# Local attention of a fused decoder: dividing the exponentials by their sums before they are turned, instead of the results after

## What is computed

```python
qkv = h @ wqkv                                  # 256 -> 3 x 512, 8 heads of 64
q = l2norm(q) * qs ; k = l2norm(k) * ksc
q, k = rotary_xpos(q, k)
# windows of 128 tokens, each looks at itself and at the window before
sim = einsum('bhwid,bhwjd->bhwij', bq * 8.0, bk)
mask = (i < j) | (i > j + WINDOW) | (j == -1)
attn = softmax(where(mask, -max, sim))
o = einsum('bhwij,bhwjd->bhwid', attn, bv)
x = x + o @ wo
```

## Time and profile before

| | us |
|---|---|
| median of 3 runs (lowest, highest) | 2656.38 (2656.29, 2656.98) |
| the profiled execution, first to last instruction | 2656.6 |
| PE busy | 2298.0 (87%) |
| DVE busy | 1419.3 (53%) |
| ACT busy | 1042.2 (39%) |
| POOL busy | 696.8 (26%) |

### The profile page before, as it was taken

How to read it: one execution, slowest core, us unless ns; L and a number is a source line. 1 busy time by engine, 2 the same in 40 slices (tenths; PEclk the granted TensorE clock), 3 DMA queues, 4 the chain that set the end, 5 groups by cost and what they waited for, 6 DMA issues and landing times. The chain is left out here.

```text
span 2656.6 us, 38842 instructions
## 1 busy us (share of the span) xinstructions
PE 2298.0 (87%) x12968; PEld 1651.9 (62%) x12968; DVE 1419.3 (53%) x4229; ACT 1042.2 (39%) x2653; POOL 696.8 (26%) x669
## 2 busy tenths in 40 slices
PE   7994499988869969995698899698999898999898
PEld 5773377765547648873387666464566675466676
DVE  3565022256658857665133666454776443677454
ACT  2443111135516610063143366343666332666432
POOL 1012311110014424412544100563433101433110
PEclk9997699979959979996799899799999999999899
DMA  9113211075000010030253211300000000000000
GB/s 232 39 72 157 85 42 51 16 164 42 1 7 1 1 42 1 19 132 28 91 172 109 94 25 33 153 1 32 1 2 1 1 1 1 1 1 1 21 24 20
DMA packets 112242, 127.38 MB, mean 48 GB/s; under 512 B 46515, under 2 KB 100021, under 8 KB 110256
## 3 DMA queue, kind: packets, MB, share of 16 engines
q1 hardware_dynamic: 103312, 103.91, 14.7%
q0 software_dynamic: 8736, 20.99, 2.2%
HBM read 79.93 MB, written 47.90 MB: 48 GB/s over the span
## 5 line engine op out<-in xcount | busy, mean ns | idle before, releaser
L461 PE MATMUL bank<-weights,work 128*128 128x256 f32 (+5 forms) x1768 | 463.1, 396 | 17.1 <-DVE weights L2542 8.1
L461 PE MATMUL bank<-work,weights 128*128 128x256 f32 (+3 forms) x1680 | 409.7, 404 | 18.1 <-DVE work L4844 10.8
L461 PEld LDWEIGHTS bank<-weights,work 128*128 128x128 f32 (+2 forms) x1768 | 314.9, 191 | 113.3 <-issue 66.1
L461 PEld LDWEIGHTS bank<-work,weights 128*128 128x128 f32 (+1 forms) x1680 | 300.0, 189 | 99.4 <-DVE work L4844 14.3
L845 POOL TENSOR_TENSOR work<-work,minus_half 128x2 f32<-128x2 f32 x96 | 69.3, 722 | 849.0 <-DVE work L838 849.0
L461 PE MATMUL bank<-weights,x_feat 128*128 128x512 f32 (+2 forms) x576 | 214.6, 507 | 15.7 <-ACT weights L4420 10.0
L870 ACT COPY x_feat<-bank 128x512 f32<-128x512 f32 x80 | 46.6, 584 | 299.2 <-PE bank L862 298.8
L461 PEld LDWEIGHTS bank<-weights,x_feat 128*128 128x128 f32 x576 | 107.8, 199 | 74.9 <-issue 49.1
L4444 ACT ACTIVATE work<-work 128x128 f32<-128x128 f32 (+1 forms) x256 | 137.0, 543 | 1.6 <-DVE work L4531 1.6
L461 PE MATMUL bank<-x_feat,weights 128*128 128x256 f32 (+3 forms) x400 | 117.9, 472 | 19.9 <-PEq L247 15.2
L1775 DVE TENSOR_TENSOR work<-bank,work 128x384 f32<-128x384 f32 (+1 forms) x64 | 31.4, 491 | 189.7 <-ACT work L1693 189.7
(11 more groups left out here) (465 smaller groups left out, 4686.7 us busy)
## 6 DMA issues: line engine op xcount, KB each, us to landing
weights<-in_weights SPq DMA_DIRECT2D x1, 12296.0 KB
weights<-in_weights SPq DMA_DIRECT2D x1, 9360.0 KB
weights<-in_weights SPq DMA_DIRECT2D x1, 8488.0 KB
work<-rows_in SPq DMA_DIRECT2D x62, 129.0 KB
rows_in<-ident SPq DMA_DIRECT2D x2, 3968.0 KB, 44.0
weights<-rows_back SPq DMA_DIRECT2D x8, 768.0 KB, 4.9
work<-rows_in SPq DMA_DIRECT2D x8, 645.0 KB, 4.2
rows_in<-ident SPq DMA_DIRECT2D x2, 2560.0 KB, 34.1
```

The lines of the kernel that those rows point to most:

```text
L461: ins = nc.tensor.matmul(out, lhsT, rhs, start=(i == 0), stop=(i == len(pairs) - 1))
```

## The change

`turn_out`, `normalise`, `turn_back` and both `store_back` are gone. In their place DVE's new `divide(u)`, one step after `exps(u)`, takes one over the sums and multiplies the exponentials in place, in two instructions (both heads' first window, 256 elements in a row, and both heads' second window, 512 elements). `turn_probs` waits for that and stands one step later, `products` too. ACT's `store_probs` copies both heads' turned exponentials. `store_out` copies the result of `products` right into `oT`. `output` and `turn_x` stand two steps earlier, and the loop has two steps fewer. The buffers `outT` and `o` are gone, and the sums have three places instead of five.

```diff
-    STEPS = UNITS + LEAD + 8
+    STEPS = UNITS + LEAD + 6
...
             def turn_probs(u):
-                pe.wait_ge(S.probs_done, u + 1)
+                pe.wait_ge(S.probs_scaled, u + 1)
                 for s in range(2):
                     if u:
                         pe.wait_ge((S.pair0_stored, S.pair1_stored)[s], u)
-                    if u >= 5:
-                        pe.wait_ge((S.back0_stored, S.back1_stored)[s], u - 4)
...
-            def turn_out(u):
...
-                for i in range(2):
-                    ins = nc.tensor.transpose(K.bank[SM[i]][:, 3 * P:4 * P], outT[:, u % 2, i * P:(i + 1) * P],
-                                              K.ident[:])
-                ins.then_inc(S.out_turned, 1)
-
-            def turn_back(u):
...
-                for i in range(2):
-                    ins = nc.tensor.transpose(K.bank[TB[i]][:, 3 * P:4 * P], o[:, u % 2, i, :], K.ident[:])
-                ins.then_inc(S.oT_done, 1)
...
             for t in range(STEPS):
-                if (u := unit_of(t - LEAD - 4)) is not None:
-                    turn_out(u)
                 if (u := unit_of(t - LEAD)) is not None:
                     scores(u)
-                if (u := unit_of(t - LEAD - 5)) is not None:
-                    turn_back(u)
-                if (u := unit_of(t - LEAD - 1)) is not None:
+                if (u := unit_of(t - LEAD - 2)) is not None:
                     turn_probs(u)
-                if (u := unit_of(t - LEAD - 2)) is not None:
+                if (u := unit_of(t - LEAD - 3)) is not None:
                     products(u)
...
             def store_probs(u):
-                a.wait_ge(S.probsT_done, 2 * u + 1)
-                if u >= 2:
-                    a.wait_ge(S.out_done, u - 1)
-                nc.scalar.copy(probsT[:, u % 2, 0, :], K.bank[TB[0]][:, 0:3 * P]).then_inc(S.pair0_stored, 1)
+                for s in range(2):
+                    a.wait_ge(S.probsT_done, 2 * u + s + 1)
+                    if u >= 2:
+                        a.wait_ge(S.out_done, u - 1)
+                    nc.scalar.copy(probsT[:, u % 2, s, :], K.bank[TB[s]][:, 0:3 * P]
+                                   ).then_inc((S.pair0_stored, S.pair1_stored)[s], 1)
...
-                nc.scalar.copy(outT[:, u % 2, :], K.bank[X][:, 0:L]).then_inc(S.outT_stored, 1)
...
+                nc.scalar.copy(oT[:, b % 2, m, :], K.bank[X][:, 0:L]).then_inc(S.outT_stored, 1)
...
+            def divide(u):
                 v.wait_ge(S.probs_done, u + 1)
-                nc.vector.reciprocal(den[:, u % 2, :, :], sums[:, u % 5, :, :]).then_inc(S.vector_step, 1)
...
+                nc.vector.reciprocal(den[:, u % 2, :, :], sums[:, u % 3, :, :]).then_inc(S.vector_step, 1)
                 v.wait_ge(S.vector_step, u + 1)
-                for i in range(2):
-                    ins = nc.vector.tensor_tensor(o[:, u % 2, i, :].rearrange("p (s d) -> p s d", s=2),
...
+                for i, at, width in blocks:
+                    ins = nc.vector.tensor_tensor(probs[:, u % 3, :, at:at + width], probs[:, u % 3, :, at:at + width],
+                                                  spread(den[:, u % 2, i, :], width), ALU.mult)
+                ins.then_inc(S.probs_scaled, 1)
```

More of the change, by code:

```diff
@@ L4213, in local_attention @@
     probs, probsT = A(3, 2, 3 * P), A(2, 2, 3 * P)
-    top, bias, sums = A(2, 2, 2), A(2, 2, 2), A(5, 2, 2)
-    outT, o, den = A(2, L), A(2, 2, P), A(2, 2, 2)
+    top, bias, sums, den = A(2, 2, 2), A(2, 2, 2), A(3, 2, 2), A(2, 2, 2)
     w = W["wqkv"][:, 2 * layer:2 * layer + 2, :]
@@ L4279, in project @@
                     pe.wait_ge(S.v_stored, n)
+                if c == 2 and i == 1 and b >= 3:
+                    pe.wait_ge(S.residual_done, b - 2)
                 if c == 2 and i == 0 and b >= 4:
-                    pe.wait_ge(S.residual_done, b - 3)
-                if c == 2 and i == 1 and b >= 4:
                     pe.wait_ge(S.xT_stored, b - 3)
@@ L4374, in turn_x @@
                 pe.wait_ge(S.residual_done, b + 1)
-                pe.wait_ge(S.v_stored, min(2 * (b + 4) + 1, TILES))
+                pe.wait_ge(S.v_stored, min(2 * (b + 3) + 2, TILES))
                 for k in range(KT):
@@ L4399, in _ @@
                     project(n, 0)
+                if (b := batch_of(t - LEAD - 7)) is not None:
+                    output(b)
                 if (b := batch_of(t - LEAD - 9)) is not None:
-                    output(b)
-                if (b := batch_of(t - LEAD - 11)) is not None:
                     turn_x(b)
@@ L4439, in exps @@
                 a.wait_ge(S.max_done, u + 1)
-                if u >= 5:
-                    a.wait_ge(S.out_stored, u - 4)
+                if u >= 3:
+                    a.wait_ge(S.probs_scaled, u - 2)
                 for s in range(2):
@@ L4479, in _ @@
                     store_q(n)
-                if (u := unit_of(t - LEAD - 1)) is not None:
+                if (u := unit_of(t - LEAD - 2)) is not None:
                     store_probs(u)
-                if (u := unit_of(t - LEAD - 5)) is not None:
-                    store_back(u)
                 if (n := tile_of(t - 1)) is not None:
@@ L4493, in _ @@
                     store_v(n)
-                if (b := batch_of(t - LEAD - 11)) is not None:
+                if (b := batch_of(t - LEAD - 9)) is not None:
                     store_x(b)
@@ L4608, in _ @@
             for t in range(STEPS):
-                if (u := unit_of(t - LEAD - 4)) is not None:
-                    normalise(u)
                 if (u := unit_of(t - LEAD)) is not None:
                     tops(u)
+                if (u := unit_of(t - LEAD - 1)) is not None:
+                    divide(u)
                 if (n := tile_of(t - 2)) is not None:
@@ L4615, in _ @@
                     rotate(n, 1)
-                if (u := unit_of(t - LEAD - 5)) is not None:
-                    store_back(u)
-                if (u := unit_of(t - LEAD - 1)) is not None:
-                    store_probs(u)
                 if (n := tile_of(t - 1)) is not None:
@@ L4622, in _ @@
                     rotate(n, 0)
-                if (b := batch_of(t - LEAD - 9)) is not None:
+                if (b := batch_of(t - LEAD - 7)) is not None:
                     residual(b)
```

49 lines of the change are left out of this document (5 added, 44 removed).

## The result

| | before | after |
|---|---|---|
| median (lowest, highest), us | 2656.34 (2655.04, 2656.98) | 2625.53 (2623.31, 2628.84) |
| after / before, 95% interval | | 0.989 (0.9876 to 0.9904) |
| span of the profiled execution | 2656.6 | 2621.6 |

What follows compares the result with a forecast made beforehand. PE was taken as the bound of steps 10 to 31 (busy 153.75 of 156.05 us). Turns 9.2, ramp 0.3 and tail 5.7 make 15.2 us a layer, 30.4 for both, off 2656.6: forecast 2626 us, range 2618 to 2637.

Steps and rivals of the forecast that it cites:

- The turns, 0.43 us for a unit: PE, steps 10 to 31: dropping both pairs of turns saves 0.43 us for each of 21.5 units, 9.2 us a layer.
- `divide`, 1.25 us: DVE: reciprocal 0.30, 256-element product 0.34 and 512-element product 0.61 make 1.25 us for each unit.
- DVE's room in the short odd step, 0.16: Short odd step: DVE's work of 5.55 us fits a step of 5.71 us, with 0.16 to spare.
- The keys' cover, 0.34: Keys through DVE and POOL: ready 8.61 us after the even step's scores, wanted by PE at 8.95, 0.34 spare.
- The first rival: Steady part: `divide` or POOL's way is longer, so PE waits for the keys; 2633 to 2641 us, chance 0.15.
- The port, 0.14 and 0.52 us free: Odd step: POOL's blocking operations end 0.14 us before DVE's bias and 0.52 before `divide`'s first product, so no collision.
- slower from about 1.1 us dearer: Odd step: bias and `divide` fall inside POOL's work if `divide` is about 1.1 us dearer; 2672 us, chance 0.04.
- The ramp, 0.3: Start of each layer: step 8 shorter by some 0.8 us, about 0.5 lost again in step 9; 0.3 us gained.
- The tail, 34.3 us, a gain of 5.7: From step 32 to the last `output`: 34.3 us where it was 39.97, a gain of 5.7 us a layer.
- Nothing behind the last `output`: From the last `output` of a layer on: no change in time.
- Larger gain: Turns worth their full start-to-start spacing, 12.0 us a layer, and a tail gain of 8; 2616 us, chance 0.08.
- no gain: DVE becomes the bound, its load in a batch rising from 21 to about 27 us; 2650 to 2656, chance 0.05.

Runs made afterwards that it cites:

- no_division: Changed kernel without the division by the sums, `turn_probs`, `products` and ACT's copies one step earlier; 2624.54 us, 0.9886 of before.
- recip_only: Changed kernel in the same order, but `divide` takes only the reciprocal and leaves out its two products; 2618.69 us, 0.9870 of before.
- dear_one: Changed kernel with `divide`'s 256-wide product made twice, 0.34 us more DVE time a unit; 2631.51 us, 0.9912 of before.
- dear_two: Changed kernel with both products of `divide` made twice, 0.95 us more DVE time a unit; 2661.34 us, 1.0028 of before.
- dear_reduce: Changed kernel with two unread reductions over the exponentials (one SBUF operand each, 0.93 us) added in `divide`; 2653.56 us, 0.9998 of before.
- divide_first: Changed kernel with DVE doing the last unit's `divide` ahead of the next `tops`, not behind it; 2632.01 us, 0.9914 of before.
- out_first: Changed kernel with ACT's `store_out` ahead of the exponentials from step 32 on; 2624.32 us, 0.9892 of before.
- keep_busy: Changed kernel plus unread identity transposes on PE in step 33, 16 before `products`, 8 before the last keys; 2622.52 us, 0.9877 of before.
- clock_fill: out_first plus 24 unread identity transposes on PE in step 33 before the last keys' `turn_qk`; 2616.42 us, 0.9863 of before.
- best_tail: out_first, DVE copying the second head's turned exponentials from unit 25, and last keys' sums and rotation before `divide` in step 32; 2621.09 us, 0.9873 of before.

## Why the prediction held

Forecast 2626.0, measured 2625.53; 30.4 us were forecast for the attention stretches and 30.0 measured. By its steps:

- **The turns, 0.43 us for a unit.** Right. Before and after differ by 9.36 and 9.34 us in the steady part, which makes 0.435 for each of the 21.5 units; the 0.56 of their spacing would have made 12.0. The short odd step is 5.71 and the even one 6.48, as forecast. Comparing whole steps with and without the turns gave the size, and the start-to-start spacing would have misled.
- **`divide`, 1.25 us.** Measured 1.15: the instruction behind the reciprocal starts 0.20 after it and not 0.30. no_division and recip_only show that it costs the steady part nothing.
- **DVE's room in the short odd step, 0.16.** Measured 0.17: there the next `tops`, at 1938.27, waited 0.17 us for the scores.
- **The keys' cover, 0.34.** 0.49, by the cheaper `divide`. The first rival, PE waiting for keys, is thereby real but not reached: dear_one, 0.34 dearer, is inside the cover, dear_two and dear_reduce are beyond it. Its price of 0.1 for each pair and each 0.1 us of excess was too small: a step with `output` takes DVE's lateness as well, most of which is the held bias, and at 0.44 of excess (dear_reduce) two pairs lose 1.70 us (0.49 and 1.21), not 0.88.
- **The port, 0.14 and 0.52 us free.** 0.24 and 0.52, and no product of the steady part is longer than it is alone. The rule of the Trainium skill (SBUF — State Buffer, Who interferes with whom) that such a pair of instructions contends is borne out in step 33 (1.87 for 1.03), divide_first (1.72 for 1.03) and dear_two (1.87). The rival built on it, *slower from about 1.1 us dearer*, had the threshold nearly right: dear_reduce, 0.93 dearer than the changed kernel and so 0.83 dearer than my price, is level with before. Its mechanism was there in part: in dear_reduce the bias stands inside POOL's work in the short odd steps, as the rival said, and adds to DVE's plain time on the keys' way. How much either would do alone no run shows.
- **The ramp, 0.3.** 0.7 and 2.0. Steps 8 and 9 give 0.64 us of it in both layers: step 8 goes from 6.48 to 5.53, and step 9 from 5.92 to 6.23, since it waits 0.45 us for POOL's keys, as foreseen (about 0.5). The rest, 0.1 and 1.4 us, lies ahead of step 8 and is not traced; I count it as chance, since the ramp runs from 49.5 us (out_first, layer 1) to 51.2 (the changed kernel, layer 0) in kernels that are the same up to step 31.
- **The tail, 34.3 us, a gain of 5.7.** The step that was off: 36.1 and 36.2, a gain of 3.5. Up to step 33 the schedule fits the trace to 0.1 us (scores 27 at 3.0, measured 3.05; last keys turned at 8.7, measured 8.79). Then the turned keys take 0.90 us to the start of `output` in place of 0.49, and `output` 4.57 to the next scores in place of 3.50: 1.5 us that the durations of the full clock don't have. keep_busy and clock_fill show that this is the clock. The other 0.3 to 0.4 comes later, piece by piece: `output` of batch 6 starts 1.7 us late, `products` of unit 31 1.9 (34.8 for 32.9). I took the clock to stay up in step 33, as it did before, where PE was idle for 1.85 of the 4 us from 2037 to 2041; now it is idle for 3.07 of the 6 from 2022 to 2028.
- **Nothing behind the last `output`.** Not so in layer 1: the last `output` of before ran there in 5.38 us (the line below), against 3.69 in the earlier trace rows, and after in 3.72, which is 1.7 us of gain that the sum didn't have. In that execution of before the granted clock was 0.50 from 2486 to 2488; it had stayed at 1.00 in layer 0 behind almost the same waits. The smaller gain in the tail (4.4 us less for both layers, 7.0 for 11.4) was made up by this, by the ramp (2.1 more) and by the steady part (0.3 more). The total was better than its terms: that it came within 0.5 us is luck, for some 3 us of what filled the gap (the fallen clock of before and the untraced part of the ramp) have nothing to do with the change.

```profile
2485.63 5.38 PE L461 MATMUL bank<-weights 128*128 128x256 f32 x16 [0.43 <-DVE weights L4561]
```

*Larger gain* (2616) and *no gain* did not come: the first needed the spacing price, the second a DVE bound, and DVE is busy for 111.38 of 146.69 us. What stays open is why the clock falls behind one wait and not behind another: the same waits lower it in one layer and not in the other (no_division, best_tail, the last `output` of before), and a wait of 1.9 us in step 33 lowers it in both layers of divide_first (the next `output` takes 4.70 and 4.73 us) and in neither of recip_only (3.62). Open too are the 2 to 6 us by which the earlier stages vary.

## What to carry to other kernels

Price work that you take from the bounding engine by whole steps that the kernel already has with and without it, and work that you add to another engine against the cover of each path that runs through it: below the cover it is free (0.34 us more here, in the steady part), beyond it the price may be more than one for one, since a late engine also hands its lateness to the next step, and comes to stand where another engine blocks it. Cover in the loop says nothing of the steps behind it: there the same 0.34 us cost 1.8 to 2.0 us a layer. Where engines wait for each other, a new wait on TensorE costs its own length and can then cost the lower clock for what follows; if the wait can't go, filling it with idle transposes gave 1.4 to 1.6 us back each time.

## What the hardware showed that was not expected

- Behind two waits of 1.91 and 0.89 us the granted clock fell to 0.56 to 0.58 for some 4 us, and cost 1.5. Behind waits of 2.69 us it fell in one layer and not in the other, with the same instructions in front; behind a single one of 1.9 us it fell in divide_first and not in recip_only.
- Plain transposes of 128 columns, 24 in 2.84 us, were enough to keep the clock at 1.00.
- An instruction of four elements a row is held by POOL like a long one (0.56 and 0.71 us in place of 0.16), and POOL is held as well: when both start together, its multiplication takes 1.32 us and not 1.04. Reductions, which read one operand in SBUF, are not held beside the same POOL work (dear_reduce, 1.01 us).
